# Decoder of two layers on one Trainium2 core: both attention stages of the second layer as one pipeline of 32 groups

## The reference

```python
x = x + _L0_attn_ref(_layernorm(x, axis=-1), ...)
x = x + _L0_xattn_ref(_layernorm(x, axis=-1), ctx_1024, ...)
x = x + _L0_ffn_ref(_layernorm(x, axis=-1), ...)
x = x + _L1_attn_ref(_layernorm(x, axis=-1), ...)
x = x + _L1_xattn_ref(_layernorm(x, axis=-1), ctx_1024, ctx_1024, mask_SxS2_bk0, ...)
x = x + _L1_ffn_ref(_layernorm(x, axis=-1), ...)
```

## Time and profile before

| | us |
|---|---|
| median of 3 executions | 1402.38 |
| the profiled execution, its own time | 1404.72 |
| its span in the profile | 1402.9 |
| PE busy in the span | 1298.8 (93%) |
| DVE busy | 975.4 (70%) |
| ACT busy | 812.0 (58%) |
| POOL busy | 452.8 (32%) |

### The profile page before, as it was taken

One profiled execution on the slowest core, in us unless ns is written; L12 is line 12 of the kernel. 1 busy time (PEld: TensorE's weight loads), 2 busy tenths in 40 slices (PEclk: granted clock), 3 DMA queues, 4 the chain that ended last, 5 costly groups with the idle time before them and its releaser, 6 DMA issues. The chain is left out here.

```text
span 1402.9 us, 40489 instructions
## 1 busy us (share of the span) xinstructions
PE 1298.8 (93%) x14996; PEld 1165.9 (83%) x14996; DVE 975.4 (70%) x2447; ACT 812.0 (58%) x1613; POOL 452.8 (32%) x550
## 2 busy tenths in 40 slices
PE   4999999889989999998999999779999998699997
PEld 4888888689979999998888888657888887589987
DVE  5788888556665455554877787557777776668885
ACT  2677776445655454544766766536666666346562
POOL 2212212022222121111000000035555554468884
PEclk9999999989999999999999999989999999899999
DMA  6000000031100000001000000020000000000000
GB/s 230 2 3 0 0 0 2 2 111 38 37 27 6 1 0 0 1 1 54 2 2 1 0 0 1 1 77 17 18 15 15 15 15 1 2 23 23 30 31 31
DMA packets 16771, 29.31 MB, mean 21 GB/s; under 512 B 3648, under 2 KB 7744, under 8 KB 16288
## 3 DMA queue, kind: packets, MB, share of 16 engines
q1 hardware_dynamic: 16672, 27.97, 6.0%
HBM read 23.77 MB, written 4.19 MB: 20 GB/s over the span
## 5 line engine op out<-in xcount | busy, mean ns | idle before, releaser
L796 ACT ACTIVATE a_probs<-a_S 128x512 f32<-128x512 f32 x384 | 205.2, 603 | 93.1 <-PE a_S L1193 52.7
L963 DVE TENSOR_REDUCE a_row_max<-a_S 128x4 bf16<-128x512 f32 (+1 forms) x384 | 245.6, 682 | 14.5 <-PE a_S L1140 13.9
L176 POOL TENSOR_TENSOR all_var_eps<-all_moments,all_ln_eps 128x2 f32<-128x2 f32 x96 | 26.8, 279 | 505.4 <-DVE all_moments L171 504.3
L752 POOL TENSOR_TENSOR a_shifts<-a_add_mask,a_row_max 128x512 bf16<-128x512 bf16 x128 | 133.0, 1062 | 115.7 <-DVE a_row_max L963 114.6
L1205 PE MATMUL a_AV<-a_probs,a_v_pad 128*32 128x128 f32 x3072 | 106.3, 280 | 14.4 <-issue 7.4
L1149 PE MATMUL a_S<-a_qm_hi,all_odd_split 32*128 32x256 f32 x1536 | 95.9, 305 | 11.0 <-DVE a_row_max L963 6.3
L1205 PEld LDWEIGHTS a_AV<-a_probs,a_v_pad 128*32 128x32 f32 x3072 | 80.2, 111 | 28.4 <-issue 8.8
L801 ACT ACTIVATE a_av_raw<-a_AV 128x512 f32<-128x512 f32 x96 | 57.4, 598 | 77.9 <-PE a_AV L1205 77.8
L1149 PEld LDWEIGHTS a_S<-a_qm_hi,all_odd_split 32*128 32x128 f32 x1536 | 70.9, 187 | 31.8 <-issue 19.7
L806 ACT ACTIVATE all_odd_split<-a_AV 128x256 fp32r<-128x256 f32 x96 | 36.9, 384 | 96.5 <-PE a_AV L1218 96.5
L104 PE MATMUL c_OUT<-all_odd_split,c_h_hi 128*128 128x256 f32 x512 | 90.5, 277 | 0.9 <-DVE all_x_res L1840 0.9
(11 more groups left out here) (292 smaller groups left out, 3939.1 us busy)
## 6 DMA issues: line engine op xcount, KB each, us to landing
all_cx<-in_ctx_turned SPq DMA_DIRECT2D x16, 256.0 KB, 2.7
all_cx<-in_ctx SPq DMA_DIRECT2D x16, 256.0 KB, 2.7
out_x<-all_x_res SPq DMA_DIRECT2D x16, 256.0 KB, 2.0
all_x_res<-in_x SPq DMA_DIRECT2D x7, 512.0 KB, 8.0
b_routed_wi<-in_L_ffn_wi_W SPq DMA_DIRECT2D x1, 1024.0 KB, 5.2
b_routed_wo<-in_L_ffn_wo_W SPq DMA_DIRECT2D x1, 1024.0 KB, 7.6
all_even_weights<-in_L_ffn_W_fc SPq DMA_DIRECT2D x1, 1024.0 KB, 5.2
all_even_weights<-in_L_ffn_W_proj SPq DMA_DIRECT2D x1, 1024.0 KB, 6.9
```

The source lines that it names most:

```text
L752: pool.tensor_tensor(shifts[:, j], add_mask[:], row_max[:, j, :].rearrange("p (h o) -> p h o", o=1).to_broadcast([P, QH, P]), ALU.subtract ...
L796: act.activation(probs[:, b * NQ + j, :], S2[j][:], ACT.Exp, scale=DH ** -0.5).then_inc(exp_ok, 1)
L963: dve.tensor_reduce(row_max[:, j, :], S1[j][:].rearrange("p (h k) -> p h k", h=QH), AXX, ALU.max).then_inc(max_ok, 1)
```

## The change

`attention_stage` takes a list of layers. For a0 the list has one; for the second layer it has two (`AttentionLayer`), and the stage runs N = 32 groups: 0 to 15 self-attention, 16 to 31 cross-attention. `at(w)` gives the layer of a group and its number in it. There is no end of a block between the layers any more. The order of every engine, and so of all three attention passes, changes with it:

- DVE: `moments_of` runs for G+4 in the second half, between `normalise_x` and `add_output` (before: G+3, in the first half). The first `low_q` runs before `low_k`, the second right behind it (rope: before `normalise` and behind it). `take_v` runs before `scaled_query`.
- POOL: `pool_rstd` runs for G+4 in the second half, behind the last shift of that half. ACT in the first half: `take_v`, or `high_q` where DVE takes the values, runs before `out_high`; in a0's second half `high_k` does too.
- First groups: mask, bias row and allowed rows of the cross layer are computed while the self-attention starts or in its group 14; in group -1 ACT makes `q_hi` and `km` before `v`, and PE's value bias of a0 comes behind the keys.
- The split of the cross layer's weights moves to the ends of both halves of groups 1 and 2; its raw weights lie where the ternary weights come later, so SP waits for the split before it loads those.
- Fold of b0: PE slots 2, 6 and 7 of group 15 (before: 6, 7 and 8).
- Ternary weights: counted from group 11 of the cross layer (before: 13); magnitudes in slots 0, 2, 4 and 6, sums and levels in slot 9, and the quantising steps in slots 11, 15, ... 39 (before: 11 to 18 without gaps). So each half group of the last four has one step, ahead of its fourth maximum.
- The hardware loops cover groups 3 to 10 of each layer.

```diff
-        if slot == STEPS - 2:
+        if slot == 2:
             self.wait_in(pe)
             pe.wait_ge(*free[0])
             self.fold(pe, banks[0], 0)
-        if slot == STEPS - 1:
+        if slot == STEPS - 2:
             pe.wait_ge(*free[1])
             self.fold(pe, banks[1], 1)
-        if slot == STEPS:
+        if slot == STEPS - 1:
             pe.wait_ge(*free[2])
             self.fold_bias(pe, banks[2])
...
-        self.first = NG - 3
+        self.first = NG - 5
...
+        n, rest = divmod(slot - STEPS - 3, 4)
+        if slot == STEPS + 1:
+            self.levels(dve, banks[1])
+        elif rest == 0 and 0 <= n < 2 * len(self.pieces):
+            self.quantise(dve, n // 2, n % 2 == 1)
...
     def schedule(eng, group):
 
         for G in range(-2, 3):
             group(G, G % 2)
-        with eng.Fori(1, (NG - 4) // 2) as i:
-            group(i * 2 + 1, 1)
-            group(i * 2 + 2, 0)
-        for G in range(NG - 3, NG + 1):
-            group(G, G % 2)
+        for n in range(len(layers)):
+            in_loop[0] = n
+            with eng.Fori(1, (NG - 6) // 2) as i:
+                group(i * 2 + (n * NG + 1), 1)
+                group(i * 2 + (n * NG + 2), 0)
+            for G in range((n + 1) * NG - 5, (n + 1) * NG + (3 if n + 1 < len(layers) else 1)):
+                group(G, G % 2)
+
+    def at(w):
+
+        n = min(max(w // NG, 0), len(layers) - 1) if isinstance(w, int) else in_loop[0]
+        return layers[n], w - n * NG
...
+    def second_piece(G, b):
+
+        return (G - 1) * PAIR + b if second is not None and isinstance(G, int) and G in (1, 2) else None
...
+            if second is not None:
+                sp.dma_start(mask_u8[:], second.mask_dram).then_inc(mask_in, 16)
+                second.wt.load(sp)
+                second.context.load_first(sp)
+                sp.wait_ge(second.wt.w_ok, len(second.wt.pieces))
                 following.load(sp)
-                if next_context is not None:
-                    next_context.load_first(sp)
+                second.context.load_rest(sp, ctx_full)
...
             def half(G, b, parity):
-                if cross and inside(G):
+                if inside(G) and at(G)[0].cross:
                     shift_step(G, b, NQ - 1)
-                if vo_bias and b == 0 and inside(G):
+                if b == 0 and inside(G) and at(G)[0].vo_bias:
                     add_bias(G)
-                if b == 0 and inside(G + 3) and not at_first(G, -2):
-                    norm.pool_rstd(pool, G + 3)
+                if rope and b == 1 and inside(G + 1):
+                    low_k(G + 1, 1 - parity)
+                if b == 1 and inside(G + 4):
+                    lay, n = at(G + 4)
+                    lay.norm.pool_rstd(pool, n)
                 for n in range(1 + next_two):
                     if b == 0 and of_next(G + 3, n):
                         next_norm.pool_rstd(pool, n)
-                if rope and b == 1 and inside(G + 1):
-                    low_k(G + 1, 1 - parity)
-                if cross and inside(G + b):
+                if inside(G + b) and at(G + b)[0].cross:
                     for j in range(NQ - 1):
                         shift_step(G + b, 1 - b, j)
...
+                if at_first(G, -1):
+                    high_q(0)
+                    masked_k(0, odd, 0)
+                    masked_k(0, odd, 1)
+                    if takes_v(0):
+                        take_v(0, odd)
+                elif inside(G + 1):
+                    if takes_v(G + 1):
+                        take_v(G + 1, odd)
+                    else:
+                        high_q(G + 1)
                 if inside(G - 1):
                     out_high((G - 1) * PAIR + 1, G - 1, 1)
                 piece(G, 1)
-                if inside(G + 1):
-                    if x_dram is not None or cross:
-                        take_v(G + 1, odd)
+                if inside(G + 1) and takes_v(G + 1) and not at_first(G, -1):
                     high_q(G + 1)
                 piece(G, 2)
-                if inside(G + 1):
+                if inside(G + 1) and not at_first(G, -1):
                     masked_k(G + 1, odd, 0)
                     if not rope:
                         masked_k(G + 1, odd, 1)
                 piece(G, 3)
+                second_weights(G, 0)
 
             def second_half(G, parity):
...
+                if rope and inside(G + 1):
+                    high_k(G + 1, odd)
                 if inside(G):
                     out_high(G * PAIR, G, 0)
                 piece(G, 5)
...
+            def value_bias(bank):
+
+                row_o = biased_layer.wt.row_o
+                dve.wait_ge(vo_full, 1)
+                for b in range(PAIR):
+                    dve.tensor_tensor(row_o[:, b, :], row_o[:, b, :], bank[:, 0:D], ALU.add).then_inc(vo_added, 1)
...
                     if rope:
                         scaled_key(G + 1)
+                        low_q(G + 1, odd, 0)
                     else:
+                        low_q(G + 1, odd, 0)
                         low_k(G + 1, odd)
-                if inside(G + 3) and not at_first(G, -2):
-                    moments_of(G + 3)
+                        low_q(G + 1, odd, 1)
                 for n in range(1 + next_two):
                     if of_next(G + 3, n):
-                        dve.wait_ge(out_free, n + 1)
+                        dve.wait_ge(out_free, N - NG + n + 1)
                         next_norm.dve_moments(dve, n)
                 if inside(G - 1):
                     normalise((G - 1) * PAIR + 1)
                 piece(G, 1)
-                if inside(G + 1):
-                    low_q(G + 1, odd, 0)
-                    if not rope:
-                        low_q(G + 1, odd, 1)
+                if rope and inside(G + 1):
+                    low_q(G + 1, odd, 1)
                 if normed_here(G + 2):
-                    norm.dve_low(dve, G + 2, FA, xT_hi[parity], xT_lo[parity])
+                    lay, n = at(G + 2)
+                    lay.norm.dve_low(dve, n, FA, lay.xT_hi[parity], lay.xT_lo[parity])
                     if x_dram is not None and is_first(G + 2):
-                        wt.prepare_dve(dve)
-                        wt.wait_in(dve)
+                        first.wt.prepare_dve(dve)
+                        first.wt.wait_in(dve)
                         moments_of(1)
-                        norm.dve_normalise(dve, 1)
+                    if x_dram is not None and at_first(G, -1):
+                        moments_of(2)
                 if last_of(G):
                     next_norm.dve_low(dve, 0, FA)
                 piece(G, 2)
                 maxima(G, 1, (G - 1) * PAIR + 1, 1)
...
+                if cross and at_first(G, -2):
+                    masks()
                 if inside(G):
                     max_step(G, 1, NQ - 1)
+                if second is not None and at_first(G, NG - 2):
+                    value_bias(S1[NQ - 1])
                 piece(G, 4)
-                if rope and inside(G + 1):
-                    low_q(G + 1, odd, 1)
-                if scaled_q and inside(G + 2):
+                if x_dram is None and inside(G + 1) and not at(G + 1)[0].cross:
+                    take_v(G + 1, odd)
+                if inside(G + 2) and at(G + 2)[0].scaled_q:
                     scaled_query(G + 2)
-                if x_dram is None and not cross and inside(G + 1):
-                    take_v(G + 1, odd)
+                if x_dram is not None and at_first(G, -2):
+                    normalise_x(1)
                 if inside(G):
                     normalise(G * PAIR)
                 piece(G, 5)
-                if cross and inside(G + 2):
-                    dve.wait_ge(ctx_hi, G + 3)
+                if inside(G + 2) and at(G + 2)[0].cross:
+                    dve.wait_ge(ctx_hi, at(G + 2)[1] + 1)
                     dve.tensor_tensor(cT_lo[:], chunked(FB), f32(cT_hi[:]), ALU.subtract).then_inc(ctx_lo, 1)
                 if inside(G + 3) and not at_first(G, -2):
-                    norm.dve_normalise(dve, G + 3)
+                    normalise_x(G + 3)
+                if inside(G + 4) and not (x_dram is not None and at_first(G, -2)):
+                    moments_of(G + 4)
                 if of_next(G + 3):
                     next_norm.dve_normalise(dve, 0)
                 if of_next(G + 2, 1):
...
+                masked = at(G)[0].cross
+                if second is not None and at_first(G, NG - 1) and b == 0:
+                    pe.wait_ge(vo_added, PAIR)
+                if at_first(G, N - 4) and b == 1:
+                    following.wait_taken(pe)
...
+                if second is not None and at_first(G, NG - 2):
+                    pe.wait_ge(max_ok, step(G, 1, NQ))
+                    second.wt.wait_split(pe)
+                    value_bias(S1[NQ - 1])
                 piece(G, 4)
-                if cross and inside(G + 2):
```

(8 more changed lines are left out.)

324 lines of the change are left out of this document (179 added, 145 removed).

## The result

The changed kernel takes 1363.2 us (median of 6 runs, 1359.54 to 1365.26). The kernel before took 1402.93 us beside it (6 runs, 1399.34 to 1406.92). The ratio is 0.9709, with a 95% interval of 0.9685 to 0.9733. The change makes the kernel 39.7 us faster; the forecast was 17.8. The direction was right, but the gain is more than twice the forecast one. The range, 1363 to 1398, holds the result by 0.2 us.

A forecast was written before the change was run, and what follows sets the result against it. PE, busy 93% of the span, was taken as the bound, leaving its 104 us idle and half-clock stretches to win. Terms -23.3 - 7 + 1.8 + 2.4 + 16.5 + 0 - 8.2 = -17.8 us gave 1384.6 us, range 1363 to 1398.

The forecast's parts named there:

- The seam: Between self- and cross-attention, groups 12 to 16: one pipeline replaces drain and fill, 72.6 us for 95.93, -23.3 us.
- The plain groups: Self-attention groups of the second layer: PE's 0.57 us wait before the queries goes, 0.5 for each of 14, -7 us.
- The split: Cross layer's weights split in both halves of groups 1 and 2: one ACT and one DVE instruction each, +2.4 us.
- The cross groups: Cross-attention groups: moments delay the scores and low_q collides with POOL's shifts, 1.5 us a group over 11 intervals, +16.5 us.
- Rival A: Cross groups: the moved DVE steps cost nothing there; 1366.7 us, chance 25%.
- The start of the second layer: Masks and moments of group 2 come before low_k of group 0, on which PE's values wait; +1.8 us.
- The end: Second layer's tail, groups 27 to 31: savings on magnitudes and levels balance the quantising steps' delays, 0 us (-5 to +5).
- a0: First attention pass: steady groups -3.2, value bias behind the keys at the start -2.5, earlier fold at the end -2.5; -8.2 us.
- rival C: Cross groups: PE's waits make the granted clock fall, each fall at least 5 us; slower, 1405 us or more, chance 8%.

The follow-up runs named there:

- e10: Changed kernel with low_q and moments of the second layer's plain groups back in their old places; 1370.96 us, 0.9772.
- e12: e3 plus two unused statistics instructions on DVE ahead of the add in each cross group; 1354.14 us, one run.
- e2: Changed kernel with both low_q of the cross layer back behind the normalisation, moments left in the chain; 1355.62 us, 0.9674.
- e1: Changed kernel with the cross layer's moments back in the first half, ahead of the normalisation, low_q left early; 1352.93 us, 0.9640.
- e7: Changed kernel with the fold of b0's weights back in slots 6, 7 and 8, behind a0's last group; 1364.35 us, 0.9742.
- e8: Changed kernel with the magnitudes and the eight quantising steps back in their old slots; 1363.59 us, 0.9734.
- e15: Changed kernel with ACT making the high part of a0's keys behind that of the output again; 1371.89 us, one run.
- e6: Changed kernel with a0's value bias ahead of the first scores on PE and between the halves on DVE again; 1363.76 us, 0.9726.
- e3: Changed kernel with both moments and low_q of the cross layer back where they were; 1351.21 us, 0.9636.
- e13: Changed kernel with ACT's old order in a0's first group: values copied before queries' high part, keys' second half masked in second half; 1360.79 us, one run.
- e14: Changed kernel with all three moves at a0's start undone (DVE's order, value bias, ACT's order); 1368.33 us, one run.
- e5: Changed kernel with a0's moments of groups 1 and 2 and normalisation of group 1 back in their old DVE places; 1364.02 us, 0.9735.
- e11: e3 plus one unused statistics instruction on DVE ahead of the add in each cross group; 1355.60 us, one run.
- e9: e3 with the second layer's masks and moments of group 2 moved to the start of group -1's second half; 1348.93 us, 0.9631.

## Why the prediction was right or wrong

**The seam** (-23.3, measured -25.1) was right in size and cause. The longest interval, 18.95 us, is 4.3 above a plain one, where the forecast had 4.5. No run undoes the seam; this is read from the two traces, with PE's idle time down by 17.0 us and the clock at 1.00 instead of 0.91.

**The plain groups** (-7, measured -7.5 with the split of the weights in it) were right: the wait for L217 went, and e10 brings it back. **The split** was mis-sized: +2.4 forecast. The intervals that hold its pieces, group 0 to 2, are 14.75 and 14.54 us, the later ones 14.6 to 14.9, so it costs nothing that can be seen. The duration of the earlier trace rows was right to take; that it fits into time in which DVE waits is likely, not shown.

**The cross groups** are the step that failed. The forecast had "the scores come 0.7 us late" and "I take one such delay of 0.45 us, plus 0.35 because the first shift starts later", 1.5 us a group. The runs show 0.86 in all, and of that 0.45 for the moments alone. There are two errors in it. "Slack: about 0.15 us" was read between two neighbours, the third maximum and the scores. The slack that counts is that of the whole loop, and e12 and e2 put it at some 0.55 us. And the second cost was added to the first, although `low_q`'s is 0.42 us with the moments there and 0.03 without. That is 8.3 us of the 23.4 by which the sum was off. Rival A, which held both to be free, was wrong by as much on the other side. Its sum, 1366.7 us, comes nearest to the result, but only because the other terms were too small as well, and the lower edge of the range was set to reach it: that the range holds the result is luck.

The rule of the Trainium skill (SBUF — State Buffer, Who interferes with whom), that a DVE instruction with two SBUF inputs and a GpSimd instruction that reads SBUF exclude each other for their whole length, agrees with the traces in kind, and nearly in size. In the changed kernel the first `low_q` begins just ahead of a shift; it takes its usual 0.74 us, and four shifts take 4.52 us where they take 4.04 in e2 with no `low_q` beside them. In the steady group of e1 shown above, where both begin within 0.1 us of each other, `low_q` takes 1.63 us, 0.89 more than alone, beside a shift of 1.04. The second `low_q` and `add_bias`, side by side, took 1.47 and 1.54 us where they take 0.74 and 1.10 apart. What failed is the step from there to the time. The extra 3 us that I had put at the rule's door did not come, since a delay of this size costs a group 0.03 us without the moments and 0.42 with them.

**The start of the second layer** (+1.8): +3.1 in this profile. The forecast priced waits, and PE's idle time grew by 0.4 us only (0.7 in e7); the rest is the clock, which stood at 0.92. In thirteen profiles with this start the stretch is longer by 0.7 us where the clock stayed at 1.00, 1.9 to 2.0 at 0.96 and 2.8 to 3.1 at 0.92. So the size of the term was met in some of them, by something that it didn't hold.

**The end** (0, measured -4.3): the step that failed is the charge of "6.5 in all" for eight quantising steps between the third and the fourth maximum, with "2.0 for magnitudes". PE's waits for POOL come to 4.4 us (1.03, 0.25, 1.05, 0.60, 0.29, 0.60 and 0.60), and the magnitudes lie ahead of this stretch, where they cost 0.8 us (e8). The "some 9 above the pace" to be balanced is 7.3 by the adds of the kernel before: the three intervals of 20.63, 17.66 and 20.40 us against 17.2, and the last, 7.81, against the 7.55 of a1. Kernel e8 shows that the spreading gains, some 3 us at the same clock.

**a0** (-8.2, measured -16.5). The steady part was right in cause and size: -3.2 for -4.0 (e15). The end was right in cause (the fold, e7), and its 2.5 us are what PE's idle time lost, 2.4. The other 2.0 of the 4.4 are PE's busy time, with the clock at 0.97 instead of 0.87: the forecast put the clock at nothing. The start is the second step that failed. I priced the value bias (2.5) and not the moments of group 2, which the change puts behind the low part of group 1: PE's queries waited 2.93 us there and wait 0.24 now, and the clock is 1.00 up to the first add instead of 0.94. The value bias itself shows nothing beyond the spread (e6). The first add came 5.6 us earlier than my term.

Of the 23.4 us in all, 8.3 are the cross groups, 5.6 a0's start, 4.3 the end, 2.9 the plain groups with the split, 1.9 a0's end, 1.8 the seam and 0.8 a0's steady part; 0.6 the last stretch; the two stretches with longer times than forecast, b0 with c0 and the start of the second layer, give back 2.7. The 1.4 us of b0 and c0 mean nothing: over all kernels here, which share this code, the stretch takes 367.1 to 371.2 us. Almost all errors have one sign. I had priced waits that the new order makes, only a part of the waits that it takes away, and outside the seam nowhere the clock.

## What to carry to other kernels

A delay in a chain costs only what it exceeds the slack of the whole loop by, and the distance between two neighbouring instructions in the trace is not that slack; dummy instructions of known length in the chain measure it, once one of them is long enough to show (0.34 us cost nothing here, 0.67 us did). Costs in one loop need not add: undo each alone and both together before you price them. Read the granted clock of a stretch before you put its time down to an order: here 1 to 2 us between executions of the same code were the clock. And the same reordering can be worth 0.67 us in one kind of group and cost 0.86 in the other, so where one program runs two kinds of groups, choose the order for each: with the cross layer's order of before in the common pipeline, the kernel takes 1351.21 us, and with the masks moved as well 1348.93.

## What was not expected of the hardware

The clock fell where PE had waited, and it did so in some executions and not in others of the same code. At the start of the second layer PE waits 3.04 or 3.05 us in the changed kernel and in the twelve others that have this start. From the last add of c0 to the first of the layer they take:

| granted clock in the stretch | kernels | us |
|---|---|---|
| 1.00 | e7 | 39.73 |
| 0.96 | e1, e2, e3, e6, e8, e13, e14 | 40.88 to 40.96 |
| 0.92 | changed, e5, e11, e12, e15 | 41.76 to 42.07 |

So the same wait left the clock alone once and lowered it twelve times, by two different amounts, and the time follows the clock to 0.3 us. That also answers rival C's "at least the 5 us" of a fall: 0.96 over 40.9 us is an estimated 3.3 us at 1.2 GHz. In e9 the waiting time is cut into 0.86, 0.81 and 1.55 us, and the clock did not fall there; since it did not in e7 either, this is a hint and not a measurement.
